# Twelve steps instead of sixteen: two short query tiles of causal attention joined into one step

## The chip, the core and the metric

The kernel runs on one core of a Trainium2 chip. The metric is the device time in microseconds, median of several runs.

## What is computed

The program is two transformer-like layers over 8 batches of 512 tokens of width 128, all in fp32: a recurrent layer with a quantised feed-forward, then an attention with 16 heads and a gated cell. The change lies in the attention of the second layer, whose core is:

```python
nq = _rms(x @ w_cq, g_qnorm)
q = concat(q_nope, rope(q_rope))                       # 16 heads of 96
k1 = concat(ckv @ w_dk_nope, rope(x @ w_krope)/16)     # latent keys
ks, vs = keys and values of the 32 selected tokens
kw, vw = x @ w_wink (rotated), x @ w_winv              # "window" keys
a1 = _attn(q, k1, v1, causal=True)
a2 = _attn(q, ks, vs, causal=False)
a3 = _attn(q, kw, vw, causal=True)
out = (g[:, 0] * a1 + g[:, 1] * a2 + g[:, 2] * a3) @ w_proj
```

A causal softmax over 512 tokens is computed twice per head (a1 and a3), a small one over 32 selected tokens once (a2).

## The kernel before

Heads go in groups of four (HG), so a batch has four groups, and the kernel has 32. The first group runs on its own (FIRST), then a hardware loop of seven turns with four groups each (FULL: groups 1, 2, 3 of a batch and group 0 of the next), then the last three (LAST). Each group has two *rows* (a = 0: a1, a = 1: a3), and each row has 16 *units*: one head h and one query tile t of 128 queries. Tile t sees (t+1) x 128 keys. A row first runs tiles 3 and 2 of its four heads in turn (the tall half), then tiles 1 and 0 (the low half). In row 0, tiles 2, 1 and 0 also compute 32 scores against the selected keys (those of tile 3 ride with tile 0).

Every engine walks through the same numbered steps; step s of PE, DVE and ACT belongs to unit s, with older units at fixed lags, and semaphores join them. What the engines do in step s:

- PE (`attend`, from L1593): the scores of unit s (L1650, L1652) into one of three banks, after the maximum or the exponential of unit s-3; then, at some steps, one set of value matmuls for four heads (`values`, L1612; PV_TALL and PV_LOW say when: four sets for the tall half, two for the low one), or the spreading of the inverted row sums (`spread`, L1623, step SPREAD); then the transposes of unit s-2 (L1672), after its exponential and after the move of unit s-4, whose bank they take; then a *task*, if one is planned.
- DVE (from L1271): a DVE-read task, the masked row maximum of unit s (L1341, which also copies the scores to Pb), the move of unit s-3 out of its bank to PT (L1349, if its tile is moved by DVE), then pieces of the rows (INVERT L1303, NORM L1313, ADD L1322), of the selected softmax (L1282 to L1300), and of the batch.
- ACT (from L875): an ACT-read task, the move of unit s-2 (L886, tile 2 only), the copy of selected scores (L899), the exponential of unit s with its sum (L903), and the move of the spread inverses (L909, step MOVE).

MOVER says who moves which tile: DVE tiles 3, 1 and 0, ACT tile 2. T_LAG is 2, D_LAG is 3.

Tasks share one PSUM bank (7): `group_tasks` (L73) lists at which step of a group which one is filled: nine projections for the next group (x1q, x2q, nq, x1k, x2k, nk3, nk1, vw, vl), the transposed selected probabilities p2T, their product o2, the output projection op of the group before, and for one group in four those of the batch (z4T, gf, gi, gc; cqkv, kr, sel, ks, nqT; vs). A task waits until the one before has been read, and its reader reads it at the start of the next step. POOL rotates queries and keys (`rope`, L633), repeats the inverted row sums (L676), and SP lays the parts of queries and keys with small DMAs (L499). The step numbers of all this were written by hand.

Of the kernel before, what the change touches and what calls it, by code (L numbers as in the profile page):

```python
# [15 lines left out]
P = 128  # L16
B, T = 8, 512
NT = T // P
# [28 lines left out]
HALVES = ((3, 2), (1, 0))  # L47


def units(groups):  # L50

    return [(q, h, a, t) for q in range(groups) for a in range(2) for half in HALVES for h in range(HG) for t in half]

# [19 lines left out]
def group_tasks(q, g, last=False, first=False):  # L73

    steps, proj, extra = {"op": 12, "p2T": 22, "o2": 24}, (0, 2, 4, 7, 8, 13, 15, 17, 19), []
    if g == 0:
        steps, proj = {"op": 11, "p2T": 23, "o2": 25}, (1, 2, 4, 7, 8, 13, 15, 27, 30)
        extra = [] if first else [(17, "z4T"), (20, "gf"), (21, "gi"), (24, "gc")]
    if g == 2 and not last:
        steps, proj = {"op": 11, "p2T": 22, "o2": 24}, (1, 2, 4, 7, 8, 13, 14, 16, 17)  # L80
        extra = [(19, "cqkv"), (23, "kr"), (27, "sel"), (28, "ks"), (30, "nqT")]
    if g == 3 and not last:
        steps, proj = {"op": 11, "p2T": 22, "o2": 24}, (2, 3, 6, 7, 9, 13, 15, 17, 19)
        extra = [(27, "vs")]
# [23 lines left out]
class Turn:  # L108
# [3 lines left out]
    def __init__(self, tasks, i=0):  # L112
# [18 lines left out]
        self.c0 = (NG - 1) * GU if self.first else 0  # L131
# [19 lines left out]
    def col(self, s):  # L151

        q, h, a, t = self.units[s]
        return self.c0 + s - s % RU + (NT - 1 - t) * HG + h
# [10 lines left out]
    def half_free(self, k):  # L165

        r = self.r0 + k // RU
        return r * 2 - 1 if self.units[k][3] >= 2 else r * 2

    def moved(self, k, who):  # L170

        per = sum(MOVER[u[3]] == who for u in units(1))
        if k < 0:
            return self.p0 * per - sum(MOVER[u[3]] == who for u in units(1)[k + 1 + GU:])
        return self.p0 * per + sum(MOVER[u[3]] == who for u in self.units[:k + 1])
# [31 lines left out]
def build(nc, wide_d, mods_d, lat_d, row_d, x_d, out_d):  # L207
    with ExitStack() as ctx:
# [111 lines left out]
        nmax = cv(NG * GU)  # L320
        lsum = cv(NG * GU)
# [147 lines left out]
        def turned(turn, k):  # L469

            _, h, _, t = turn.units[k]
            low, at = int(t < 2), (t % 2 == 0) * P
            return PT[low][:, h, at:].rearrange("p (c x) -> p c x", x=P)[:, 0:2 * t + 1:2]

        def turned_bank(turn, k):
            t = turn.units[k][3]
            return bank[3 + k % 2][:, 0:(t + 1) * P].rearrange("p (c x) -> p c x", x=P)
# [273 lines left out]
        def _(act):  # L751
# [123 lines left out]
            def attend(turn):  # L875
                n_units, u0 = len(turn.units), turn.u0
                p2h = p2.rearrange("p (t j k) -> p j t k", t=NT, j=HG)
                for s in range(turn.n1):
# [4 lines left out]
                    if turn.n0 <= k < n_units and MOVER[turn.units[k][3]] == "act":  # L883
# [3 lines left out]
                    if s < n_units:  # L887
                        q, h, a, t = turn.units[s]
                        n, lo = (t + 1) * P, scores_at(a, t)
                        act.wait_ge(s_max, u0 + (s + 1))  # L890
                        if lo:

                            if turn.g(q) == 1 and s % GU == 1:

                                act.wait_ge(s_c, turn.b + 1)
                            tiles = slice(0, NT, NT - 1) if t == 0 else slice(t, t + 1)
                            m = 2 if t == 0 else 1
                            scores = bank[turn.score_bank(s)][:, 0:m * (KEEP + P)].rearrange("p (m x) -> p m x", m=m)[:, :, 0:KEEP]
                            made = A(p2h[:, h, tiles], scores, ACT.Copy)  # L899
                            if h == HG - 1 and t == 0:  # L900
                                made.then_inc(s_s2, 1)
                        c = turn.col(s)
                        A(Pb[:, s % 4, 0:n], Pb[:, s % 4, 0:n], ACT.Exp, bias=nmax[:, s:s + 1], scale=-1.0,  # L903
                          accum_out=lsum[:, c:c + 1]).then_inc(s_p, 1)
# [5 lines left out]
                    if s < n_units and s % GU == 18:  # L910
                        act.wait_ge(s_s2m, turn.p0 + (s // GU + 1))
                        A(p2, p2, ACT.Exp).then_inc(s_p2, 1)
                    if s < n_units and s % GU == 24 and ("nq", s // GU + 1) in turn.index:
                        selected_keys(turn, s // GU + 1)
# [25 lines left out]
        def _(v):  # L940
# [330 lines left out]
            def attend(turn):  # L1271
# [31 lines left out]
                def row_inverted(r):  # L1303
# [5 lines left out]
                    step(v.reciprocal(inv[:, r % 2], lsum[:, turn.c0 + r * RU:turn.c0 + (r + 1) * RU] if r >= 0 else lsum[:, NG * GU - RU:]))  # L1309
# [19 lines left out]
                for s in range(turn.n1):  # L1329
# [3 lines left out]
                    if s < n_units:  # L1333
                        _, _, a, t = turn.units[s]
                        n, lo = (t + 1) * P, scores_at(a, t)
                        v.wait_ge(s_qk, u0 + (s + 1))
                        if not (turn.first and s < 4):
# [3 lines left out]
                        v.tensor_tensor_reduce(Pb[:, s % 4, 0:n], bank[turn.score_bank(s)][:, lo:lo + n], w("mask", T - n), -1.0, 3e38,  # L1341
                                               ALU.add, ALU.min, nmax[:, s:s + 1]).then_inc(s_max, 1)
                    k = s - D_LAG
                    if turn.n0 <= k < n_units and MOVER[turn.units[k][3]] == "dve":
# [12 lines left out]
                    g = turn.g(q)  # L1357
                    if at == 17:
                        selected_shifted(q)
                    if at == 19:  # L1360
# [418 lines left out]
```

## Time and profile before

| | |
|---|---|
| median of 3 runs | 2321.69 us (2316.57 to 2322.24) |
| profiled execution | 2312.3 us, its span 2310.5 us |
| PE busy | 1911.7 us, 83% |
| DVE busy | 1367.5 us, 59% |
| ACT busy | 1163.8 us, 50% |
| POOL busy | 645.1 us, 28% |
| mean granted TensorE clock | 0.900 |

Busy times overlap between engines. A matmul's end in the trace is modelled, so back-to-back matmuls seem to overlap. "Idle before" is the gap on an engine in front of an instruction, with what ended it.

### The profile page before, as it was taken

What the parts mean: (1) busy time and instruction counts of PE and PEld (TensorE: products, weight loads), DVE (VectorE), ACT (ScalarE), POOL (GpSimd) and SP (SyncE); (2) the same over time, 40 slices, a digit from 0 to 9 for tenths busy, and PEclk for the clock granted to TensorE, in tenths of its full rate; (3) what the DMA queues carried; (4) which work ended last, traced back from release to release, by engine and by line L of the source; (5) the groups of instructions that cost most, each with busy time, mean ns of one, the idle gap of its engine ahead of it and who ended that gap; (6) DMA issues with size and microseconds to landing.
All of it is one profiled execution on the core that took longest, in us unless ns stands there. A gap on an engine that the chain in (4) does not pass through costs nothing.

```text
span 2310.5 us, 40290 instructions
## 1 busy us (share of the span) xinstructions
PE 1911.7 (83%) x10620; PEld 1069.9 (46%) x10620; DVE 1367.5 (59%) x4228; ACT 1163.8 (50%) x3476; POOL 645.1 (28%) x659
## 2 busy tenths in 40 slices
PE   3433357999899998999899989999899899989985
PEld 2221224555445544555455545555455455545542
DVE  5999833656555555555555555555565655565563
ACT  1112213656556565556465655565565556556651
POOL 0323233323323332323232322323232323332200
PEclk7556556999999998989998999899998999899998
DMA  3000002111101110111111111111111111111101
GB/s 137 0 0 0 0 14 53 44 41 36 51 19 40 35 50 23 36 32 40 36 34 36 42 43 33 33 46 42 34 33 45 42 34 33 35 52 31 35 1 37
DMA packets 71349, 81.44 MB, mean 35 GB/s; under 512 B 29521, under 2 KB 37842, under 8 KB 70994
## 3 DMA queue, kind: packets, MB, share of 16 engines
q1 hardware_dynamic: 71122, 78.74, 13.2%
q8 instruction: 102, 1.67, 0.3%
q14 instruction: 125, 1.02, 0.1%
HBM read 7.90 MB, written 2.10 MB: 4 GB/s over the span
## 4 chain that ended last, share of the span: by engine, by line
PE 69%; DVE 17%; issue 8%; ACT 3%; DVEq 1%; POOL 1%; SPq 1%; DMA 0%; ACTq 0%; POOLq 0%
PE bank L1652 21%; PE bank L1672 14%; PE bank L1612 9%; DVE arena L1349 4%; PE bank L1522 4%; PE bank L1523 4%; DVE arena L1341 3%; PE bank L1623 2%; PE bank L1564 2%; PE bank L1545 2%; PE bank L1518 1%; PE bank L1577 1%; PE bank L1560 1%; DVE arena L1106 1%; PE bank L1585 1%
## 5 line engine op out<-in xcount | busy, mean ns | idle before, releaser
L1341 DVE CUSTOM_DVE_ANT_0 arena<-bank,W 128x512 f32<-128x512 f32 (+3 forms) x1024 | 502.0, 490 | 711.4 <-PE bank L1652 573.4
L1652 PE MATMUL bank<-arena 96*128 96x512 f32 (+6 forms) x2048 | 785.6, 466 | 30.8 <-issue 18.3
L903 ACT ACTIVATE arena<-arena 128x512 f32<-128x512 f32 (+3 forms) x1024 | 572.8, 559 | 442.5 <-DVE arena L1341 439.2
L1672 PE MATMUL bank<-W,arena 128*128 128x128 f32 x2560 | 487.1, 288 | 97.1 <-DVE arena L1349 92.0
L1672 PEld LDWEIGHTS bank<-W,arena 128*128 128x128 f32 x2560 | 306.2, 142 | 464.3 <-DVE arena L1349 226.0
L1652 PEld LDWEIGHTS bank<-arena 96*128 96x128 f32 x2048 | 341.1, 199 | 174.6 <-issue 149.7
L1349 DVE COPY arena<-bank 128x512 f32<-128x512 f32 (+2 forms) x768 | 356.2, 464 | 2.0 <-issue 1.5
L685 POOL TENSOR_TENSOR arena<-arena,one 128x512 f32<-128x512 f32 x64 | 66.7, 1042 | 950.6 <-DVE arena L1311 939.7
L1612 PE MATMUL bank<-arena 128*32 128x256 f32 (+1 forms) x3072 | 227.6, 369 | 8.3 <-DVE arena L1349 7.7
L903 ACT ACTIVATION_READ_ACCUMULATOR arena<-arena 128x1 f32 x1024 | 194.8, 190 | 0.0
L886 ACT ACTIVATE arena<-bank 128x384 f32<-128x384 f32 x256 | 125.6, 491 | 116.2 <-PE bank L1672 116.0
L899 ACT ACTIVATE arena<-bank 128x32 f32<-128x32 f32 (+1 forms) x384 | 78.9, 206 | 153.2 <-DVE arena L1341 152.4
L636 POOL TENSOR_TENSOR arena<-arena,W 128x512 f32<-128x512 f32 x64 | 69.8, 1091 | 272.7 <-ACT arena L828 272.7
L1473 PE MATMUL bank<-W,arena 128*128 128x128 f32 x160 | 37.5, 379 | 122.2 <-ACT arena L786 52.7
L1612 PEld LDWEIGHTS bank<-arena 128*32 128x32 f32 x3072 | 61.5, 110 | 166.0 <-issue 128.2
L1522 PE MATMUL bank<-arena,LW 96*128 96x512 f32 x192 | 109.2, 652 | 2.1 <-ACT arena L828 1.4
L1523 PE MATMUL bank<-arena,W 128*128 128x512 f32 x192 | 103.9, 623 | 5.0 <-ACT arena L828 3.6
L645 POOL TENSOR_TENSOR arena<-arena 128x512 f32<-128x512 f32 x64 | 81.4, 1271 | 39.0 <-DMA arena<-arena 31.9
L1473 PEld LDWEIGHTS bank<-W,arena 128*128 128x128 f32 x160 | 26.3, 195 | 135.3 <-ACT arena L786 54.3
L828 ACT ACTIVATE arena<-bank 128x512 f32<-128x512 f32 x128 | 75.6, 590 | 23.5 <-PE bank L1523 8.2
L1341 DVE DVE_READ_ACCUMULATOR2_ANT arena<- 128x1 f32 x1024 | 85.1, 83 | 0.0
L649 POOL TENSOR_TENSOR arena<-arena 128x512 f32<-128x512 f32 x64 | 81.3, 1270 | 5.0
(260 smaller groups left out, 2259.3 us busy)
## 6 DMA issues: line engine op xcount, KB each, us to landing
arena<-arena SPq DMA_DIRECT2D x896, 64.0 KB, 2.0
arena<-arena SPq DMA_DIRECT2D x64, 128.0 KB, 2.4
W<-wide SPq DMA_DIRECT2D x1, 3730.0 KB, 13.3
X<-x SPq DMA_DIRECT2D x8, 256.0 KB, 5.5
out<-arena SPq DMA_DIRECT2D x8, 256.0 KB, 2.2
arena<-arena SPq DMA_DIRECT2D x96, 16.0 KB, 1.9
LW<-lat SPq DMA_DIRECT2D x1, 768.5 KB, 14.3
arena<-mods SPq DMA_DIRECT2D x1, 768.0 KB, 4.5
```

Source lines behind the costliest of these rows:

```text
L645: step(pool.tensor_tensor(stX1, rt[:, 2], rt[:, 3], ALU.subtract))
L649: pool.tensor_tensor(stX2, rt[:, 0], rt[:, 1], ALU.add).then_inc(s_rope, 1)
L886: A(turned(turn, k), turned_bank(turn, k), ACT.Copy).then_inc(s_pa, 1)
L899: made = A(p2h[:, h, tiles], scores, ACT.Copy)
L903: A(Pb[:, s % 4, 0:n], Pb[:, s % 4, 0:n], ACT.Exp, bias=nmax[:, s:s + 1], scale=-1.0, accum_out=lsum[:, c:c + 1]).then_inc(s_p, 1)
L1341: v.tensor_tensor_reduce(Pb[:, s % 4, 0:n], bank[turn.score_bank(s)][:, lo:lo + n], w("mask", T - n), -1.0, 3e38, ALU.add, ALU.min, nmax[: ...
L1349: CP(turned(turn, k), turned_bank(turn, k)).then_inc(s_pd, 1)
L1522: return MM(dst[:], LW[0:QL, col:col + P], latT[0:QL], start=True, stop=True)
L1523: return MM(dst[:], w("wink", col, P), hTc, start=True, stop=True)
L1612: last = MM(bank[5][rows, low * 2 * P:low * 2 * P + n], V[a][turn.g(q) % 2][:, c, rows], PT[low][:, h, c * 2 * P:c * 2 * P + n], start=(c ...
L1652: MM(bank[turn.score_bank(s)][:, 0:lo + n], query(t), Kb[a][0:QD, g % 2, h, skip:skip + lo + n], start=True, stop=True).then_inc(s_qk, 1)
L1672: last = pe.transpose(bank[3 + k % 2][:, c * P:(c + 1) * P], Pb[:, k % 4, c * P:(c + 1) * P], ident)
```

## The change

Tiles 1 and 0 of a head become one unit: their scores lie side by side in one bank (`laid`), two maxima and two exponentials follow each other in its step, its three transposed blocks are put in an order that lets one copy of 384 elements move them, and tile 2 is now moved by DVE as well, so that ACT moves none. A row has 12 steps and a group 24. The lag of the DVE move is two steps instead of three. The steps of value matmuls, row pieces and all tasks are numbered anew.

```diff
-HALVES = ((3, 2), (1, 0))
+STEPS = ((3,), (2,)), ((1, 0),)
...
+def laid(a, tiles):
+
+    at, out = 0, []
+    for t in reversed(tiles):
+        lo = scores_at(a, t)
+        out.append((t, (t + 1) * P, lo, at))
+        at += lo + (t + 1) * P + (lo if t == 0 else 0)
+    return out[::-1]
...
-T_LAG, D_LAG = 2, 3
-PV_TALL, PV_LOW = 11, 19
-INVERT, SPREAD, MOVE, NORM, ADD = 16, 19, 21, 23, 24
-MOVER = {3: "dve", 2: "act", 1: "dve", 0: "dve"}
+T_LAG, D_LAG = 2, 2
+PV_TALL, PV_LOW = 10, 14
+INVERT, SPREAD, MOVE, NORM, ADD = 12, 14, 15, 16, 17
+MOVER = {3: "dve", 2: "dve", 1: "dve"}
...
-    steps, proj, extra = {"op": 12, "p2T": 22, "o2": 24}, (0, 2, 4, 7, 8, 13, 15, 17, 19), []
+    steps, proj, extra = {"op": 8, "p2T": 18, "o2": 20}, (0, 2, 4, 6, 7, 9, 11, 13, 15), []
     if g == 0:
-        steps, proj = {"op": 11, "p2T": 23, "o2": 25}, (1, 2, 4, 7, 8, 13, 15, 27, 30)
-        extra = [] if first else [(17, "z4T"), (20, "gf"), (21, "gi"), (24, "gc")]
+        steps, proj = {"op": 7, "p2T": 18, "o2": 20}, (0, 1, 3, 5, 6, 9, 10, 21, 22)
+        extra = [] if first else [(12, "z4T"), (14, "gf"), (15, "gi"), (19, "gc")]
     if g == 2 and not last:
-        steps, proj = {"op": 11, "p2T": 22, "o2": 24}, (1, 2, 4, 7, 8, 13, 14, 16, 17)
-        extra = [(19, "cqkv"), (23, "kr"), (27, "sel"), (28, "ks"), (30, "nqT")]
+        proj = (0, 1, 3, 5, 6, 9, 10, 11, 12)
+        extra = [(15, "cqkv"), (17, "kr"), (19, "sel"), (21, "ks"), (22, "nqT")]
...
         def turned(turn, k):
 
-            _, h, _, t = turn.units[k]
-            low, at = int(t < 2), (t % 2 == 0) * P
-            return PT[low][:, h, at:].rearrange("p (c x) -> p c x", x=P)[:, 0:2 * t + 1:2]
+            _, h, _, tiles = turn.units[k]
+            if tiles[0] == 1:
+                return PT[1][:, h]
...
# ACT, step s
+                        for t, n, lo, at in laid(a, tiles):
+                            c = turn.col(s, t)
+                            here = Pb[:, s % 4, at_p:at_p + n]
+                            done = A(here, here, ACT.Exp, bias=nmax[:, c:c + 1], scale=-1.0, accum_out=lsum[:, c:c + 1])
+                            at_p += n
+                        done.then_inc(s_p, 1)
...
# PE, step s
+                        for t, n, lo, at in laid(a, tiles):
+                            skip = 0 if lo or a else KEEP
+                            last = MM(B_[:, at:at + lo + n], query(t), Kb[a][0:QD, g % 2, h, skip:skip + lo + n],
+                                      start=True, stop=True)
...
-                        for c in range(t + 1):
-                            last = pe.transpose(bank[3 + k % 2][:, c * P:(c + 1) * P], Pb[:, k % 4, c * P:(c + 1) * P], ident)
+                        order = (0, 2, 1) if tiles[0] == 1 else range(tiles[0] + 1)
+                        for n, c in enumerate(order):
+                            last = pe.transpose(bank[3 + k % 2][:, n * P:(n + 1) * P], Pb[:, k % 4, c * P:(c + 1) * P], ident)
```

On DVE the selected softmax moves from steps 17, 19, 20, 21 to 13, 15, 16, 17; for the batch, the tokens from 20 to 23 to 13 to 16, the picks (L1220) from 24 to 17, norm_latents from 28 to 20, the statistics from 13 to 9, normed_out (L1252) from 16 to 11, the cell from 26 to 29 to 21 to 23.

## Rows read from the trace of the kernel before

**Rows 1.** The row maxima by their line: count, shortest/median/longest ns, first and last start.

```profile
L1341 DVE CUSTOM_DVE_ANT_0 arena<-bank,W x1024: 282/485/693, 379.8 to 2255.5; 128x512 f32<-128x512 f32 x86, 128x256 f32<-128x256 f32 x85
```

**Rows 2.** Four groups of a turn: us; busy PE, PEld, DVE, ACT, POOL; clock.

```profile
1143.70:1199.10 55.40, 51.65 (x302) 28.29 (x302) 31.21 (x103) 32.53 (x98) 15.65 (x14) 0.96 0.14 34
1199.10:1265.60 66.50, 61.78 (x349) 36.96 (x348) 36.98 (x120) 36.40 (x119) 21.91 (x20) 0.90 0.12 30
1265.60:1319.70 54.10, 50.52 (x311) 27.69 (x309) 31.48 (x103) 33.46 (x102) 15.64 (x14) 1.00 0.20 47
1319.70:1384.50 64.80, 57.52 (x316) 31.42 (x316) 36.72 (x123) 34.91 (x102) 18.36 (x20) 0.94 0.14 38
```

**Rows 3.** The chain of waits in the third group (1265.6 to 1319.7), shares by line.

```profile
by line: PE bank L1652 26.1%; PE bank L1672 20.1%; PE bank L1612 11.2%; issue 7.5%; DVE arena L1349 6.4%; PE bank L1523 4.8%; PE bank L1522 4.8%; DVE arena L1341 4.3%; PE bank L1623 2.2%; PE bank L1564 2.0%; PE bank L1518 1.9%; PE bank L156
```

**Rows 4.** Waits of one turn (1143.7 to 1384.5): us in total, times, longest.

```profile
PE bank L1672 <- DVE arena L1349: 11.2, 23, 2.3
...
PE bank L1652 <- issue: 3.0, 1, 3.0
```

**Rows 5.** Timeline of PE in the third group: start, us, instructions, idle before.

```profile
1302.17 0.81 PE L1652 MATMUL bank<-arena 96*128 96x384 f32 x2
1302.82 0.49 PE L1672 MATMUL bank<-W,arena 128*128 128x128 f32 x3
1303.15 1.02 PE L1652 MATMUL bank<-arena 96*128 96x512 f32 x2
...
1311.52 0.44 PE L1672 MATMUL bank<-W,arena 128*128 128x128 f32 x2 [1.11 <-DVE arena L1349]
...
1312.11 0.64 PE L1612 MATMUL bank<-arena 128*32 128x256 f32 x8
1312.68 0.33 PE L1672 MATMUL bank<-W,arena 128*128 128x128 f32 x1
```

**Rows 6.** Groups of instructions by shape, third group: busy us, mean ns, idle before.

```profile
L1672 PE MATMUL bank<-W,arena 128*128 128x128 f32 x81 | 15.3, 285 | 2.9 <-DVE arena L1349 2.8
...
L1341 DVE CUSTOM_DVE_ANT_0 arena<-bank,W 128x512 f32<-128x512 f32 x9 | 6.2, 690 | 7.5 <-PE bank L1652 4.5 <-PE bank L1672 2.9
L903 ACT ACTIVATION_READ_ACCUMULATOR arena<-arena 128x1 f32 x32 | 6.1, 189 | 0.0
...
L1349 DVE COPY arena<-bank 128x512 f32<-128x512 f32 x8 | 5.5, 686 | 0.0
...
L903 ACT ACTIVATE arena<-arena 128x256 f32<-128x256 f32 x8 | 4.0, 504 | 2.3 <-DVE arena L1341 2.2
L886 ACT ACTIVATE arena<-bank 128x384 f32<-128x384 f32 x8 | 3.9, 490 | 3.3 <-PE bank L1672 3.3
...
L1341 DVE CUSTOM_DVE_ANT_0 arena<-bank,W 128x256 f32<-128x256 f32 x8 | 3.4, 422 | 3.7 <-PE bank L1652 3.7
L1349 DVE COPY arena<-bank 128x256 f32<-128x256 f32 x8 | 3.4, 420 | 0.0
...
L903 ACT ACTIVATE arena<-arena 128x128 f32<-128x128 f32 x8 | 3.2, 397 | 1.3 <-DVE arena L1341 1.3
...
L1341 DVE CUSTOM_DVE_ANT_0 arena<-bank,W 128x128 f32<-128x128 f32 x8 | 2.3, 292 | 3.7 <-PE bank L1652 2.8 <-PE bank L1672 0.9
L1349 DVE COPY arena<-bank 128x128 f32<-128x128 f32 x8 | 2.3, 286 | 0.1
```

**Rows 7.** Timeline of POOL in the first group: the two rotations.

```profile
1150.68 1.09 POOL L636 TENSOR_TENSOR arena<-arena,W 128x512 f32<-128x512 f32 x1 [4.57 <-ACT arena L828]
...
1156.46 1.28 POOL L649 TENSOR_TENSOR arena<-arena 128x512 f32<-128x512 f32 x1
...
1164.93 1.27 POOL L645 TENSOR_TENSOR arena<-arena 128x512 f32<-128x512 f32 x1 [0.48 <-DMA arena<-arena]
```

**Rows 8.** Timeline: the picks of the second group, z4T of the fourth.

```profile
1244.18 2.42 DVE L1220 TENSOR_SCALAR arena<-W,rankT 128x32 f32<-128x32 f32 x4
...
1351.33 0.63 PE L1473 MATMUL bank<-W,arena 128*128 128x128 f32 x4 [2.15 <-DVE arena L1252]
```

More of the change, by code:

```diff
@@ L469, in turned @@
         def turned(turn, k):
[L471 to L473 removed]
+            _, h, _, tiles = turn.units[k]
+            if tiles[0] == 1:
+                return PT[1][:, h]
+            return PT[0][:, h, (tiles[0] == 2) * P:].rearrange("p (c x) -> p c x", x=P)[:, 0:2 * tiles[0] + 1:2]
         def turned_bank(turn, k):
[L476 to L477 removed]
+            tiles = turn.units[k][3]
+            blocks = bank[3 + k % 2][:, 0:sum(t + 1 for t in tiles) * P]
+            return blocks if tiles[0] == 1 else blocks.rearrange("p (c x) -> p c x", x=P)
         block = ctx.enter_context(nc.Block())
@@ L882, in attend @@
                     k = s - T_LAG
-                    if turn.n0 <= k < n_units and MOVER[turn.units[k][3]] == "act":
+                    if turn.n0 <= k < n_units and MOVER[turn.units[k][3][0]] == "act":
                         act.wait_ge(s_pT, u0 + (k + 1))
@@ L1333, in attend @@
                     if s < n_units:
-                        _, _, a, t = turn.units[s]
-                        n, lo = (t + 1) * P, scores_at(a, t)
+                        _, _, a, tiles = turn.units[s]
                         v.wait_ge(s_qk, u0 + (s + 1))
@@ L1340, in attend @@
                         v.sem_inc(s_seen, 1)
-                        v.tensor_tensor_reduce(Pb[:, s % 4, 0:n], bank[turn.score_bank(s)][:, lo:lo + n], w("mask", T - n), -1.0, 3e38,
-                                               ALU.add, ALU.min, nmax[:, s:s + 1]).then_inc(s_max, 1)
+                        at_p = 0
+                        for t, n, lo, at in laid(a, tiles):
+                            c = turn.col(s, t)
+                            last = v.tensor_tensor_reduce(Pb[:, s % 4, at_p:at_p + n],
+                                                          bank[turn.score_bank(s)][:, at + lo:at + lo + n],
+                                                          w("mask", T - n), -1.0, 3e38, ALU.add, ALU.min, nmax[:, c:c + 1])
+                            at_p += n
+                        last.then_inc(s_max, 1)
                     k = s - D_LAG
-                    if turn.n0 <= k < n_units and MOVER[turn.units[k][3]] == "dve":
+                    if turn.n0 <= k < n_units and MOVER[turn.units[k][3][0]] == "dve":
                         v.wait_ge(s_pT, u0 + (k + 1))
@@ L1627, in attend @@
                     if s < n_units:
-                        q, h, a, t = turn.units[s]
-                        g, n = turn.g(q), (t + 1) * P
+                        q, h, a, tiles = turn.units[s]
+                        g = turn.g(q)
                         if s % GU == 0:
```

118 lines of the change are left out of this document (59 added, 59 removed).

## The prediction

> **What bounds the kernel now.** I read the page first: PE is busy 83% of the span, DVE 59%, ACT 50%. That makes TensorE the suspect, but a busy PE is a modelled figure, so I asked where the row maxima of the attention run. They run from 379.8 to 2255.5 us, 1024 of them [rows 1]: 1876 of the 2310.5 us are the stage the change touches. I then cut one turn of the batch loop at the first row maximum of each group of heads [rows 2]. The four groups last 55.4, 66.5, 54.1 and 64.8 us, sum 240.8. The second also prepares the next batch's selected tokens and latents, the fourth runs the layer norm and the cell; the first and third are plain. The third is the cleanest: granted clock 1.00 throughout, PE 50.5 of 54.1 us, DVE only 31.5, ACT 33.5.
>
> So is the plain group bound by matmuls? Its chain of waits says: mostly. Lines of PE carry it, but DVE L1349 (moving a turned block) has 6.4%, DVE L1341 (the row maximum) 4.3% and "issue" 7.5% [rows 3]. Together that is 18.2% of 54.1, or 9.8 us in which the path leaves PE. The waits of the whole turn show the shape: the transposes of L1672 wait for the move of L1349, 23 times and 11.2 us, the longest 2.3 [rows 4]. The timeline shows one of them: 1.11 us of idle PE in front of two transposes, ended by L1349 [rows 5].
>
> Why do they wait? Transposed blocks go to two banks in turn, so the transposes of unit k need the move of k-2. PE issues the transposes of k in step k+2; VectorE moves k-2 in step k+1, behind the maximum of k+1. PE thus has one score matmul between the maximum's input and its own need, VectorE a maximum and a move: 0.69 + 0.69 us for a 512-wide tile [rows 6]. Any odd piece on VectorE goes straight to PE.
>
> **The change, part by part.**
>
> Steps. A row of attention (4 heads, 4 query tiles) goes from 16 steps to 12, a group from 32 to 24. Score columns, transposes, value matmuls and their weights stay the same in number and size, so PE's own work stays. Within a joined step two maxima and two exponentials follow each other; their number stays too. What goes is 8 rounds of waits per group.
>
> Moves. Per head and row VectorE had 512, 256 and 128 elements: 0.686 + 0.420 + 0.286 = 1.39 us, ScalarE 384 in 0.490 [rows 6]. Now VectorE moves 512, 384 and 384. No DVE copy of 384 stands in the trace. The three sizes lie on a line of 0.153 us plus 1.04 ns an element, which gives 0.55; the bounds are the 256 and the 512 copy, 0.42 and 0.69. The new sum is 0.686 + 2 x 0.55 = 1.79, +0.40, and with eight head-rows +3.2 us of VectorE per group (1.1 to 5.4 by the bounds). VectorE goes from 31.5 to 34.7 us in a plain group, ScalarE (eight moves less) from 33.5 to 29.5. Neither is full.
> The Trainium skill (VectorE: DVE Perf Modes, its section on the TRN2 errata) prices a VectorE pass out of PSUM at 120 cycles plus one per element at 0.96 GHz. An estimate from it is 0.525 us for 384, which would lower VectorE's load by 16 x 0.03 = 0.4 us per group against my line; no row here has the size.
>
> The lag. The move of k-2 now runs in step k, a step earlier, and PE needs it in step k+2: a whole step lies between. The transposes' waits for L1349 should go. In the plain group, idle PE in front of L1672 is 2.9 us [rows 6]. But a modelled matmul end lies later than the next one could start: scores began at 1302.17 and are drawn 0.81 long, yet the transposes behind them began at 1302.82 [rows 5], so each wait hides 0.16 us more. With some nine waits, those of values and p2T among them (some 0.5 us, an estimate from the 1.11 of a long one), that is 2.9 + 0.5 + 9 x 0.16 = 4.8 us. Shorter waits hide wholly in that tail; the chain's 9.8 us is the bound for all, and I take 1.6 us of the remaining 5.0. Gone: 6.4 us a group, bounds 2.9 and 9.8.
>
> What is late next. I laid the 24 steps of a plain group end to end, in the order of the code's waits. PE's prices come from start to start in the timeline [rows 5]: 384 columns of scores 0.65 us, so 1.69 ns a column, 0.86 for tile 3 or a projection, 0.70 or 0.65 for tile 2; three transposes 0.33, so 0.11 each; values of 256 columns 0.57. A joined unit has 480 or 384 columns, 0.81 or 0.65; its short matmuls need as many weight loads as long ones, so I take 0.95 and 0.75.
> - Steps 16 to 18. VectorE has a maximum and a move in each (1.38, 1.12, 1.38 us), in 16 also the row's normalisation and a small reciprocal, in 17 the scaling of the selected probabilities; a pass over 512 is 0.69 by the nearest rows, the small one I take at 0.3 [rows 6]. With step 16's scores issued at 0, the scaling ends near 5.5; p2T, which needs it, stands in step 18, where PE arrives at 4.0. Wait about 1.6 us.
> - Steps 21 and 22. The tall values of the second row now begin the step after their last move. In 21 VectorE first adds o2 (0.69), then takes a joined maximum (0.42 + 0.29) and the move (0.55); PE, with no task in 21, arrives about 1.2 us early. The first row has nk3 in step 9 as cover and waits for nothing.
> - Step 7. x2k follows x1k directly. ScalarE reads x1k only when POOL has finished the rotation of q, 7.1 us from its first operation to the end of its last [rows 7], and that starts no earlier than now: about 0.6 us. Low values in step 2: 0.1.
> Together 3.5 us; with sequencer gaps on VectorE, which I did not lay, 4.1. Bounds: zero, if PE's own seams cover them, and 8 us.
> Joined steps lengthen the way from scores to probabilities: 0.42 + 0.29 on VectorE, then 0.50 + 0.19 + 0.40 + 0.19 on ScalarE [rows 6], some 3.9 us with the selected scores and the handovers. Two steps of PE, with the third's scores in front, give 4.1 us at the barest place (steps 20 to 22). It just holds.
> POOL, SP and DMA: the second rotation still waits for the laid parts of the first (its store at 1164.93, 7.2 us after the first ended at 1157.74 [rows 7]) and ends near 27 us, before the repeat of the row sums (28) and the spread (30). The lays end near 39 us of a group of 52. No wait.
>
> Odd groups. In the second, the four picks of 2.42 us [rows 8] move from step 24 to 17, beside the scaling; cqkv, kr, p2T, sel, o2, ks and nqT share one bank in eight steps. Their readers sit in ScalarE's and VectorE's order, and VectorE still waits in line for ks. In the fourth, z4T still waits for normed_out (2.15 us now [rows 8]) and VectorE reaches it some 0.8 us before POOL's deviation is there. The loop's turn costs PE 3.0 us [rows 4] as before. The new waits on banks at a loop's start ask for one unit more than they must; the units asked for are long done. I take 2 us gained in each, as the same transposes' waits go.
>
> The sum: plain group 6.4 - 4.1 = 2.3 us, odd group 2.0 to 2.3; over 32 groups 32 x 2.3 = 74 us. The profiled execution took 2312.3 us (span 2310.5) and the median of the runs is 2321.7, 9 us more. A difference carries over: span near 2237, and 2321.7 - 74 = **2248 us**.
>
> **The rivals.**
> *The new waits are covered.* Everything named under "late next" was laid without PE's small seams; if PE is 0.15 us later per step, p2T and the values find their inputs. Then 4.5 to 5 us a group stay: 32 x 4.6 = 147, **2175 us**. For it: VectorE and ScalarE both stay under 70%. There is also clock to win: the second group ran at a mean grant of 0.90, the first and fourth at 0.96 and 0.94 [rows 2], the lower of 1.2 and 2.4 GHz in the thin stretches. Against it: DVE work is now in fewer, fuller steps.
> *Slower: VectorE in series with PE.* VectorE takes the maximum of s, then sits in the move of s-2 until PE has issued that unit's transposes in the same step, and only then can take the maximum of s+1; move and values also tie PE to it in 22, 23 and 14. In steps 12 to 23 VectorE has about 20 us of work where PE has 21. If a handover costs 0.25 us on each of two instructions more in these twelve steps, that is 3 us a group over my 4.1, and with the packed bank 7 of the odd groups the account turns: it decides once the new waits pass 6.4 us. At 7.0 us: +0.6 x 32 = 19, **2341 us**.
> The Trainium skill (Perfetto Trace Analysis, the section on optimizing Scalar/DVE operations) speaks for this one: it says that grouping helps where the engine is saturated, but that where unsaturated engines cause bubbles on another, breaking instructions up may let work finish sooner. The trace agrees with its premise (DVE 58% busy in a plain group); the change goes the other way, and by the rule the latency would be worth more than the rounds saved.
> *Nothing moves:* the stall leaves L1349 and comes back at p2T and the values in full, **2322 us**.
>
> **How the numbers follow.** My sum, 2215 to 2285: 0.54. Covered waits, 2160 to 2215: 0.22. No change: 0.08. Slower: 0.16. Times under 2175 and over 2330 take some 0.18 of it, so the range is 2175 to 2330. A measurement tells 0.3% (7 us) from no change. Faster 0.77, same 0.07, slower 0.16.
>
> **What would show it.** In the new trace, transposes waiting for the move should be nearly gone, with waits in front of p2T's transposes and of the second row's first values in their place; a plain group near 51.8 us; DVE copies of 384 near 0.55 us; DVE near 35 us a group; no copy by ScalarE from the transposed banks. I am wrong if plain groups stay at 54 or more with VectorE waiting for transposes (series), or if ScalarE's exponentials, not the maximum or the move, end PE's waits (the latency of joined steps). The odd groups are the weakest part: I laid them by likeness only.

## The result, and the profile after

The changed kernel takes 2165.0 us (median of four runs, 2152.5 to 2174.9) against 2322.0 for the kernel before: a ratio of 0.933, 95% interval 0.928 to 0.938. The forecast was 2248, with a range from 2175 to 2330. The sign was right; the gain, 157 us, is twice the 74 forecast. The profiled spans differ by 147 us (2310.5 and 2163.4).

The first part of the page, then the row maxima by line (to set beside [rows 1]):

```profile
span 2163.4 us, 38682 instructions
PE 1812.5 (84%) x10620; PEld 1073.2 (50%) x10620; DVE 1465.2 (68%) x4228; ACT 1029.9 (48%) x3220; POOL 654.4 (30%) x659
...
L1364 DVE CUSTOM_DVE_ANT_0 arena<-bank,W x1024: 284/460/695, 380.1 to 2106.8; 128x512 f32<-128x512 f32 x86, 128x256 f32<-128x256 f32 x85
```

The attention stage (first to last start of a row maximum) went from 1875.8 to 1726.7 us, 149 less, so all of the gain lies there. One turn cut at the first row maximum of each group, with the columns of [rows 2] (us; busy PE, PEld, DVE, ACT, POOL; clock; DMA share; GB/s):

```profile
1087.45:1138.70 51.25, 47.88 (x297) 28.06 (x296) 35.36 (x102) 28.20 (x90) 15.97 (x14) 0.97 0.15 38
1138.70:1198.00 59.30, 57.12 (x356) 35.56 (x348) 38.31 (x119) 32.35 (x111) 21.92 (x20) 0.94 0.14 34
1198.00:1249.50 51.50, 47.90 (x316) 28.51 (x308) 35.40 (x102) 29.39 (x94) 15.99 (x14) 1.00 0.21 49
1249.50:1308.90 59.40, 54.46 (x327) 31.47 (x320) 39.47 (x123) 30.89 (x94) 18.82 (x20) 1.00 0.15 42
```

Here is the surprise. The third group, the plain one on which the prediction was built, went from 54.1 to 51.5: the forecast was 51.8. The second lost 7.2 us and the fourth 5.4, where "2 us gained in each" was forecast. The waits of PE in the third group (total us, times, longest) are the three that the prediction named, and none for the move in front of a transpose, where [rows 4] had 23 in a turn:

```profile
PE bank L1549 <- ACT arena L844: 1.5, 1, 1.5
PE bank L1595 <- DVE arena L1320: 1.3, 1, 1.3
PE bank L1638 <- DVE arena L1375: 0.7, 1, 0.7
```

VectorE's shapes in the same group show the new copy of 384 at 555 ns:

```profile
L1375 DVE COPY arena<-bank 128x384 f32<-128x384 f32 x16 | 8.9, 555 | 2.0 <-PE bank L1702 1.8
...
L1375 DVE COPY arena<-bank 128x512 f32<-128x512 f32 x8 | 5.5, 687 | 1.6 <-PE bank L1702 1.6
```

The picks and the pieces of normed_out over the whole run, before (L1220, L1252) and after (L1241, L1273); mean ns is the second number behind the bar:

```profile
L1220 DVE TENSOR_SCALAR arena<-W,rankT 128x32 f32<-128x32 f32 x32 | 17.6, 615 | 0.0
L1252 DVE TENSOR_SCALAR arena<-X,small 128x128 f32 x28 | 14.4, 575 | 0.0
```

```profile
L1273 DVE TENSOR_SCALAR arena<-X,small 128x128 f32 x28 | 7.7, 340 | 0.0
...
L1241 DVE TENSOR_SCALAR arena<-W,rankT 128x32 f32<-128x32 f32 x32 | 5.4, 233 | 0.0
```

The same instructions on the same shapes take 0.38 and 0.59 of their former time, though nothing was done to them but to move them. The clock changed as well: 0.90 became 0.94 in the second group, 0.94 became 1.00 in the fourth. A mean of 0.90 over a group says that TensorE ran a fifth of it at 1.2 instead of 2.4 GHz; such time is called half clock below.

The theory that I took from this: three causes add up. The lag removes a wait in every group; picks and normed_out no longer meet GpSimd (POOL); and the clock, which fell behind those stalls, holds. Rivals: the joined steps themselves pay more than I laid, or the bunches of small instructions were the trouble, not where they stood.

### The profile page after: what moved, and what is told of

Its sections match the earlier page's. It is cut to its first block, busy times and chain, and to the rows that moved or that the text cites. A ratio compares the mean times of both kernels' runs of the same rounds, so it can differ in the third digit from the quotient of the medians.

```text
span 2163.4 us, 38682 instructions
## 1 busy us (share of the span) xinstructions
PE 1812.5 (84%) x10620; PEld 1073.2 (50%) x10620; DVE 1465.2 (68%) x4228; ACT 1029.9 (48%) x3220; POOL 654.4 (30%) x659
## 4 chain that ended last, share of the span: by engine, by line
PE 64%; DVE 14%; issue 13%; POOL 4%; ACT 3%; SPq 1%; DMA 0%; DVEq 0%; POOLq 0%; ACTq 0%
PE bank L1675 21%; PE bank L1702 11%; PE bank L1638 8%; PE bank L1548 3%; PE bank L1549 3%; DVE arena L1364 2%; PE bank L1649 2%; PE bank L1590 1%; PE bank L1586 1%; PE bank L1544 1%; PE bank L1603 1%; DVE arena L1127 1%; DVE arena L1375 1%; PE bank L1611 1%; PE bank L1612 1%
## 5 line engine op out<-in xcount | busy, mean ns | idle before, releaser
L1364 DVE CUSTOM_DVE_ANT_0 arena<-bank,W 128x512 f32<-128x512 f32 (+3 forms) x1024 | 480.2, 487 | 437.9 <-PE bank L1675 297.5
L1675 PE MATMUL bank<-arena 96*128 96x512 f32 (+6 forms) x2048 | 718.9, 453 | 24.2 <-issue 14.7
L1375 DVE COPY arena<-bank 128x384 f32<-128x384 f32 (+1 forms) x768 | 460.1, 599 | 90.2 <-PE bank L1702 83.0
L1675 PEld LDWEIGHTS bank<-arena 96*128 96x128 f32 x2048 | 353.0, 193 | 200.9 <-issue 172.5
L1702 PE MATMUL bank<-W,arena 128*128 128x128 f32 x2560 | 428.3, 281 | 0.7 <-ACT arena L923 0.6
L1702 PEld LDWEIGHTS bank<-W,arena 128*128 128x128 f32 x2560 | 300.3, 143 | 220.3 <-issue 187.3
L1638 PE MATMUL bank<-arena 128*32 128x256 f32 (+1 forms) x3072 | 220.8, 360 | 13.2 <-DVE arena L1375 10.4
L917 ACT ACTIVATE arena<-bank 128x32 f32<-128x32 f32 (+1 forms) x384 | 65.1, 204 | 200.6 <-DVE arena L1364 199.7
L1638 PEld LDWEIGHTS bank<-arena 128*32 128x32 f32 x3072 | 60.9, 108 | 196.7 <-issue 154.9
L1499 PE MATMUL bank<-W,arena 128*128 128x128 f32 x160 | 36.4, 369 | 107.4 <-ACT arena L802 52.8
L661 POOL TENSOR_TENSOR arena<-arena 128x512 f32<-128x512 f32 x64 | 81.6, 1274 | 48.0 <-DMA arena<-arena 42.8
L665 POOL TENSOR_TENSOR arena<-arena 128x512 f32<-128x512 f32 x64 | 85.9, 1342 | 5.0
L1499 PEld LDWEIGHTS bank<-W,arena 128*128 128x128 f32 x160 | 24.9, 187 | 120.1 <-ACT arena L802 54.4
L601 POOL TENSOR_TENSOR small<-small,epsc 128x4 f32<-128x4 f32 x24 | 4.9, 203 | 219.0 <-DVE small L977 219.0
```

The source lines that it names most:

```text
L661: step(pool.tensor_tensor(stX1, rt[:, 2], rt[:, 3], ALU.subtract))
L665: pool.tensor_tensor(stX2, rt[:, 0], rt[:, 1], ALU.add).then_inc(s_rope, 1)
L1364: last = v.tensor_tensor_reduce(Pb[:, s % 4, at_p:at_p + n], bank[turn.score_bank(s)][:, at + lo:at + lo + n], w("mask", T - n), -1.0, 3e3 ...
L1375: CP(turned(turn, k), turned_bank(turn, k)).then_inc(s_pd, 1)
L1638: last = MM(bank[5][rows, low * 2 * P:low * 2 * P + n], V[a][turn.g(q) % 2][:, c, rows], PT[low][:, h, c * 2 * P:c * 2 * P + n], start=(c ...
L1675: last = MM(B_[:, at:at + lo + n], query(t), Kb[a][0:QD, g % 2, h, skip:skip + lo + n], start=True, stop=True)
```

## The experiments

All ratios are to the kernel before, run on the same chip, with 95% intervals. This table has the mean length of the four groups of a turn over the seven turns of the loop, from the starts of the row maxima in the one trace of each kernel:

| kernel | us | ratio | 1st | 2nd | 3rd | 4th |
|---|---|---|---|---|---|---|
| before | 2322.0 | 1 | 55.0 | 65.9 | 54.1 | 64.1 |
| before, lag 2 | 2181.8 | 0.939 (0.933 to 0.944) | 48.8 | 60.8 | 48.7 | 64.4 |
| before, lag 2, tile 2 by DVE | 2215.8 | 0.954 (0.951 to 0.958) | 49.3 | 63.1 | 49.8 | 64.8 |
| before, lag 2, z4T later | 2172.1 | 0.933 (0.927 to 0.938) | 49.1 | 63.9 | 48.6 | 60.5 |
| before, picks one a step | 2280.4 | 0.981 (0.979 to 0.983) | 55.0 | 61.4 | 54.1 | 64.6 |
| before, both out of POOL's way | 2261.5 | 0.974 (0.969 to 0.979) | 55.2 | 60.9 | 54.1 | 61.7 |
| before, normed_out alone | 2302.0 | 0.992 (0.989 to 0.994) | 54.9 | 67.8 | 54.1 | 61.2 |
| before, picks in another form | 2283.4 | 0.986 (0.983 to 0.989) | 55.0 | 60.1 | 54.1 | 65.0 |
| before, lag 2 and both moves | 2137.1 | 0.925 (0.918 to 0.932) | 49.0 | 58.9 | 48.7 | 59.6 |
| after | 2165.0 | 0.933 (0.928 to 0.938) | 50.7 | 58.0 | 51.8 | 59.4 |
| after, picks at 18 | 2164.5 | 0.933 (0.929 to 0.937) | 50.9 | 57.8 | 51.8 | 59.4 |
| after, tile 2 by ACT | 2129.1 | 0.917 (0.914 to 0.920) | 49.5 | 57.9 | 49.6 | 58.1 |
| after, three tasks moved | 2149.4 | 0.925 (0.923 to 0.928) | 50.3 | 58.4 | 50.1 | 59.2 |
| both of these | 2126.0 | 0.915 (0.914 to 0.917) | 49.3 | 57.7 | 49.2 | 58.2 |
| after, tile 2 by ACT, tasks anew | 2107.4 | 0.909 (0.907 to 0.911) | 48.7 | 56.8 | 48.7 | 58.3 |

### The parts of the change one by one

The kernel before with the shorter lag and nothing else:

```diff
-T_LAG, D_LAG = 2, 3
+T_LAG, D_LAG = 2, 2
```

> The kernel before with one change: VectorE moves a turned block two steps back instead of three. If the lag is the main part of the gain (theory lag), the transposes' waits for the move (11.2 us a turn of the loop before) fall under 2 us, plain groups go from 54.1 to about 51 us, and the time to 2200 to 2240 us. If the joined steps are the main part (theory join), the short steps of tiles 1 and 0 leave VectorE waiting for the transposes of the same step, plain groups stay above 53 us, and the time above 2280 us.

Measured: 2181.8 us, 140 of the 157. The third group falls by 5.4 us, the measured size of what the prediction called gone (6.4). The fourth gains nothing (64.1 to 64.4).

The same with tile 2 moved by VectorE:

```diff
-MOVER = {3: "dve", 2: "act", 1: "dve", 0: "dve"}
+MOVER = {3: "dve", 2: "dve", 1: "dve", 0: "dve"}
```

> The kernel before with the lag of two steps and with tile 2 moved by VectorE too; the steps are not joined and the tasks stay. If moving the copy to VectorE helps because ScalarE's exponentials no longer stand behind it, this is 10 to 30 us faster than the lag alone. If VectorE's extra 3 to 4 us a group cost what they free, it is within 7 us of the lag alone or slower. What is left to 2165 us is then the joined steps and the new task steps: theory join expects over 80 us left, theory lag under 50.

Measured: 2215.8, 34 us worse. The reverse edit on the changed kernel (`MOVER = {3: "dve", 2: "act", 1: "dve"}`):

> The changed kernel with tile 2 moved by ScalarE as before. If the move to VectorE was a gain, this is 10 to 30 us slower; if VectorE is what PE waits for in the groups (p2T 1.42 us, values 0.83 us a group), taking eight copies of 0.6 us off it makes this 10 to 40 us faster.

Measured: 2129.1, 36 us better. So this part of the change is a loss of 34 to 36 us in either kernel, and the prediction had it at nothing. With it on VectorE, value matmuls wait for the moves: in the unjoined kernel a wait comes up (in the whole run) that its ACT twin does not have among its longest.

```profile
PE bank L1612 <- DVE arena L1349: 25.6, 23, 1.7
```

The changed kernel with the old lag (D_LAG 3):

> The changed kernel with the move three steps back again. Theory lag: most of the gain goes, 2165 to 2240 us or more, waits of the transposes for the move come back (over 10 us a turn) and the half-clock stretches with them. Theory join: longer steps give VectorE time for either lag, under 2190 us.

Measured: ratio 1.052 (1.045 to 1.059), slower than the kernel before; the ratio is that of two runs at 2430.0 and 2454.1 us, two more took 2476.9 and 2481.6, and the trace is of one of these. The move comes a step late for the values, all over the run:

```profile
PE bank L1638 <- DVE arena L1375: 197.5, 123, 2.3
```

So the joined kernel pays only with the shorter lag. By subtraction the rest, joined steps with their newly laid tasks, brings 52 us: 2181.8 to 2129.1 with tile 2 on ScalarE, 2215.8 to 2165.0 on VectorE. The table says where: 2.9 and 6.3 us in the second and fourth group, nothing in the plain ones (0.7 and 0.9 worse).

### Is it the joining, or where the picks and normed_out stand?

First the two places one by one. The picks of the kernel before spread over steps 23 to 26:

> The kernel before with one thing changed: the four picks of the second group, 2.42 us in step 24, go one each to steps 23 to 26. Theory picks: the wait of 2.42 us in that group and the half-clock stretch of 13 to 17 us that begins 2 us later both come from this bunch; the group goes from 65.9 to about 60 us and the time falls by 35 to 50 us. Rival: the bunch is worth its own wait only, about 1.5 us a turn, 10 us in all, and the stretch of half clock stays because the small matmuls of sel and ks make it.

Measured: 2280.4, 43 less than its neighbour on the same chip (2323.9); the picks take 302 ns on average, and the second group 61.4 us. Then z4T a step later, on top of lag 2:

> The kernel before with the lag of two steps, and the task z4T of the fourth group one step later (18 instead of 17). Lag alone left the fourth group at 64.4 us while the changed kernel has 59.4; theory z4T says that the wait for normed_out (2.98 us) and the half-clock stretch behind it are that difference: the wait falls under 1 us, the group to about 61 us, the time by 15 to 30 us against the lag alone. Rival: the difference lies in the end of the loop's turn (4.1 us) and in the cell, and this kernel is within 7 us of the lag alone.

Measured: 2172.1. The 10 us under lag 2 alone are not clear of the spread (the intervals 0.927 to 0.938 and 0.933 to 0.944 overlap). In the traces the fourth group gains 3.9 us and the second loses 3.1: less waiting in one place, and more half clock in another (5.9 us a second group became 13.2). Neither run says why the picks were slow. The timeline of the kernel before does, beside [rows 8]:

```profile
1244.39 1.12 POOL L654 TENSOR_TENSOR arena<-arena,W 64x512 f32<-64x512 f32 x1 [4.79 <-ACT arena L823]
...
1245.47 1.08 POOL L655 TENSOR_TENSOR arena<-arena,W 64x512 f32<-64x512 f32 x1
```

The bunch started at 1244.18. The four picks (shortest, median, longest ns):

```profile
L1220 DVE TENSOR_SCALAR arena<-W,rankT x4: 234/656/1130, 1244.2 to 1245.5; 128x32 f32<-128x32 f32 x4
```

Two took 0.23 us, and each of the last two took as long as one GpSimd instruction. That asks for a test by place: the bunch kept together, but at a step where GpSimd is through, and normed_out likewise.

```diff
-                    if g == 2 and at == 24:
+                    if g == 2 and at == 26:
...
-                        if at == 16:
+                        if at == 15:
```

> The kernel before, with two things moved in its odd steps and nothing else: the bunch of four picks stands at step 26 instead of 24, and normed_out at step 15 instead of 16, where GpSimd has no tensor_tensor in hand at the same time. Theory (a pick or a z4 piece of VectorE is held up while GpSimd works, because the two share a way to SBUF): the bunch of picks costs 4 x 0.233 = 0.93 us instead of 2.42, the z4 pieces 340 ns instead of 575, the wait for z4T falls from 2.4 us to near nothing, the half clock behind both places shrinks, the second group takes about 60 us instead of 65.9 and the fourth about 61.5 instead of 64.1: 50 to 70 us off, 2255 to 2275. Rival (the bunch itself, or the small matmuls around it, costs the time): the pieces keep 575 ns and the picks 500 to 600, and the time stays within 15 us of 2322. If b_pick (the picks one a step, 2280) had its gain from spreading alone, this one lies above it by 20 us or more.

Measured: 2261.5 us, 57 less than its neighbour on the same chip (2318.4), and a bunch of 0.67 us. The picks, then normed_out and z4T:

```profile
1229.44 1.26 POOL L659 TENSOR_TENSOR arena<-arena 64x512 f32<-64x512 f32 x1 [0.17 <-POOL arena L655]
1230.53 0.67 DVE L1220 TENSOR_SCALAR arena<-W,rankT 128x32 f32<-128x32 f32 x4
...
1322.19 1.10 DVE L1252 TENSOR_SCALAR arena<-X,small 128x128 f32 x4
...
1325.01 0.63 PE L1473 MATMUL bank<-W,arena 128*128 128x128 f32 x4
```

The POOL row is nearly over when the picks begin, and z4T no longer waits. The time, the groups (60.9 and 61.7) and the pieces (340 ns) came as the theory had them; the bunch is shorter than its 0.93 us, because picks of 235 ns start 0.15 us apart. Place, not bunching, made them slow. normed_out alone (step 15):

> The kernel before with normed_out one step earlier (15 instead of 16) and nothing else. Theory (its pieces are held up while GpSimd works): 340 instead of 575 ns a piece, the wait for z4T in the fourth group of a turn goes from 2.4 us to 1 or less, that group takes 61.5 us instead of 64.1, and the second group stays at 65.9: 10 to 25 us off, 2295 to 2310. Rival (all of the gain of the two moves together came from the picks): within 7 us of 2320.

Measured: 2302.0, ratio 0.992 (0.989 to 0.994). So about 19 of the 57 us belong to it, and by subtraction the rest to the picks; as above, part of what the fourth group gains (2.9) goes over to the second (1.9 lost).

Then the form. Each pick of the kernel before as a tensor_tensor, at its old step:

```diff
-return TS(onehot[:, j], w("iota"), rankT[:, j, ds(b, 1)], None, ALU.is_equal)
+return TT(onehot[:, j], w("iota"), rankT[:, j, ds(b, 1)].to_broadcast([P, KEEP]), ALU.is_equal)
```

> The kernel before with the picks at their old step, but each a tensor_tensor (row of numbers against the rank, broadcast) instead of a tensor_scalar; same place, same result. It tells what of VectorE is held up while GpSimd works. If it is only the form with one tensor operand and both ends in SBUF (tensor_scalar): 220 to 300 ns a pick, the second group at 61 us, and 2275 to 2290 us in all. If any instruction of VectorE on SBUF is held up: 450 to 650 ns a pick and the time within 10 us of 2320.

Measured: 2283.4, which is what "tensor_scalar alone is held up" gave. But the trace does not say so:

```profile
L1220 DVE TENSOR_TENSOR arena<-W,rankT x4: 185/187/1083, 1235.3 to 1235.6; 128x32 f32<-128x32 f32 x4
```

The fourth pick is held up as before, 1083 ns against GpSimd's 1.13 us. The form is only shorter (0.19 us instead of 0.23), so three were through before GpSimd began, and one such wait is met instead of two. The time agreed with a theory whose mechanism is wrong; without that row I would have carried it off. The Trainium skill (SBUF — State Buffer, section "Who interferes with whom") says that VectorE and GpSimd share a pair of ports, that whichever starts first holds it for its whole instruction while the other fully blocks, and that this goes for tensor_scalar in a two-port mode and for tensor_tensor with both inputs in SBUF against GpSimd's reads. The rows above agree on both: 1130 and 1083 ns, where a GpSimd instruction took 1.08 to 1.13 us. Which port it is, no run here shows. And not every GpSimd instruction holds VectorE up. In the changed kernel with tile 2 on ScalarE all 28 picks of the loop begin while GpSimd has a power over 128x8 elements in hand (L682, drawn 1.66 us long), in its last 0.57 us, and they take 233 ns on average:

```profile
1162.13 1.66 POOL L682 TENSOR_TENSOR small<-small,cst 128x8 f32<-128x8 f32 x1
...
1163.22 0.67 DVE L1241 TENSOR_SCALAR arena<-W,rankT 128x32 f32<-128x32 f32 x4
```

So the rule of the Trainium skill, that the other fully blocks, does not show in these rows. Either the power was through with SBUF by then, or its drawn end is too late; no run tells which.

The half clock is the other half of it. These two second groups are both of the kernel before with lag 2:

```profile
475.70:534.00 58.30, 54.71 (x350) 33.24 (x349) 37.22 (x119) 35.86 (x119) 21.91 (x20) 1.00 0.14 33
697.43:761.56 64.13, 60.74 (x349) 37.77 (x349) 37.43 (x120) 36.10 (x119) 21.91 (x20) 0.89 0.13 31
```

The code is the same, and one ran (1 - 0.89) x 64.13 x 2 = 14 us at 1.2 GHz. That costs 5.8 us, 0.41 us for each us at the lower level. The kernel before gives nearly the same: its second groups took 60.9 us at a clock of 1.00 and 68.0 at 0.875. The pick experiment shows that a small stall can start it: in the second group of b_pick_tt (the picks as tensor_tensor) the bunch is 1.0 us shorter, and the group is

```profile
1190.13:1250.12 59.99, 55.69 (x349) 32.53 (x349) 35.91 (x119) 36.35 (x119) 21.92 (x20) 1.00 0.13 33
```

against 66.50 at 0.90 in [rows 2]. By 0.41, the 13 us of half clock there are 5.5 of the 6.5 us. Over the seven turns, six second groups had half clock in the kernel before (12.2 us each on average), and one in b_pick_tt (0.5).

### What joining brings by itself

Lag 2 and both moves in the unjoined kernel:

> The kernel before with D_LAG 2 and the same two moves (picks at step 26, normed_out at step 15). Theory: groups of 48.8, 58.3, 48.7 and 60.5 us, where D_LAG 2 alone had 48.8, 60.8, 48.7 and 64.4: 2115 to 2135. It says what the joined steps bring by themselves: the joined kernel with tile 2 moved by ScalarE takes 2129. If joining pays beside the better order of tasks, this one stays at 2150 or above; if the gain of the joined steps was only that their picks and z4 pieces stand elsewhere, it comes down to 2130 or below.

Measured: 2137.1, 7 us above the line I had drawn. So of the 52 us, the medians give about 45 to where the picks and normed_out stand, and 8 are left to the joined steps with their renumbered tasks (2137.1 to 2129.1). The four runs of this kernel lie 30 us apart (2131.4 to 2161.3); by the ratios, which compare with the kernel before on the same chip, it is 31 and 18 us. The first of the two is clear of noise (0.933 to 0.944 against 0.918 to 0.932); in the second the intervals overlap (0.918 to 0.932, 0.914 to 0.920): no difference is shown. The reverse test, the picks of the changed kernel at step 18, beside GpSimd:

> The kernel after with its four picks one step later, at step 18, where GpSimd works on the shared key. Theory (held up by GpSimd): the picks take 500 to 600 ns each instead of 233, a wait of 1 to 1.5 us comes up in the steps behind them, and in some of the second groups half clock with it: 10 to 50 us more, 2175 to 2215. Rival (place does not matter, the picks were slow in the kernel before for their bunching among small matmuls): 233 ns as before and within 7 us of 2165.

Measured: 2164.5, no change. The hold is there:

```profile
1183.60 1.08 POOL L670 TENSOR_TENSOR arena<-arena,W 64x512 f32<-64x512 f32 x1 [1.06 <-ACT arena L839]
1184.16 1.91 DVE L1241 TENSOR_SCALAR arena<-W,rankT 128x32 f32<-128x32 f32 x4
...
1186.21 1.05 PE L1568 MATMUL bank<-arena 128*128 128x32 f32 x8 [1.00 <-DVE arena L1241]
```

The bunch takes 1.91 us again, and sel waits 1.0 us for it. Yet the second groups last 57.8 us on average against 58.0. This one, at a clock of 1.00, took 56.6, and the changed kernel's second groups at 1.00 took 56.2: the hold by itself costs 0.4 us. Four of seven second groups had half clock in the changed kernel (59.3 us each), three of seven here. My expectation of 10 to 50 us was wrong: held-up picks cost much only where the clock falls behind them. What makes it fall here, or not, is open. It also means that the 45 us hold for the unjoined kernel alone: in the joined one the place of the picks is worth nothing that can be measured, and normed_out was not put back.

Last, the waits that the joined kernel made for itself. In the groups 1 and 3, p2T at 19, o2 at 21, x2k at 8 and op at 7, in the changed kernel and then with tile 2 on ScalarE:

> The changed kernel with task steps of the two plain groups of a turn altered: p2T 18 to 19, o2 20 to 21, x2k 7 to 8, op 8 to 7. If the new waits at p2T (1.42 us) and x2k (1.61 us) are what the prediction took them for, they mostly go: plain groups from 51.4 to about 48.7 us, the time by 16 x 2.7 = 43 us to about 2120. If VectorE paces the plain groups, the waits only move to the values or the transposes and the time stays within 10 us.

> The changed kernel with tile 2 moved by ScalarE and the same task steps altered. The waits at p2T and x2k are 0.96 and 1.17 us there: if they go, plain groups fall from 49.6 to about 47.7 us and the time by 25 to 35 us from 2129 to about 2100. If they only move, within 7 us of 2129.

Measured: 2149.4 and 2126.0. The first gains 16 us, the second 3, inside the noise: with ScalarE moving tile 2, VectorE reaches p2T's input in time anyway. The wait for x2k only went on to the task behind it, op (22.6 us in the first of the two runs, 15.9 in the second):

```profile
PE bank L1606 <- ACT arena L847: 22.6, 15, 1.5
```

So op went in front of x1k, and the odd groups were laid anew too:

> The kernel after with tile 2 moved by ScalarE and tasks laid anew: in the plain groups, op at step 6, x1k 7, x2k 8, p2T 19, o2 21, and in the odd ones p2T 19, o2 21, vw 20, vl 22 and gc 18. Theory (what the joined step left are waits for x2k, p2T and the values, each for a result that VectorE gets to late): the waits for x2k 1.6 and p2T 1.4 us go, a plain group takes 48.3 us instead of 51.8 (of which 2.3 are tile 2), the odd ones about 57: 2090 to 2110. Rival (the waits only move to the next task, as op did when x2k was laid later): within 7 us of 2126.

Measured: 2099.1; it is left out of the table, because it computes something else. In this order gc writes its result over the selected probabilities before p2T has read them, so part of the selected attention is computed from other values; the instructions are the same. With p2T and gc in their old order:

> As the last version (tile 2 moved by ScalarE, tasks laid anew), but in the groups with the output tasks p2T stays at step 18 and gc at 19, since gc's result goes where p2T still reads its input; o2 21, vw 20 and vl 22 as there. Theory (the waits for x2k, p2T and the values were the joined step's own): the plain groups take 48.5 us and the odd ones 56.6 and 57.3, 2095 to 2105 us, 25 us below the version with only three tasks moved (2126). Rival (the waits only move on): within 7 us of 2126.

Measured: 2107.4, ratio 0.909 (0.907 to 0.911), the best kernel of the study, 58 us under the changed one; this was 2 us above what I expected. Its turn:

```profile
1065.09:1114.01 48.92, 48.40 (x300) 28.79 (x300) 30.96 (x94) 31.10 (x98) 16.08 (x14) 0.98 0.16 39
1114.01:1170.12 56.11, 54.01 (x356) 33.49 (x348) 34.56 (x112) 35.37 (x119) 21.90 (x20) 1.00 0.14 35
1170.12:1218.87 48.75, 48.13 (x316) 28.53 (x308) 31.21 (x94) 32.15 (x102) 16.09 (x14) 1.00 0.22 53
1218.87:1277.60 58.73, 54.82 (x324) 31.15 (x316) 35.59 (x115) 33.86 (x102) 18.78 (x20) 0.98 0.16 42
```

It is 30 us under the best unjoined kernel, but that one's tasks were not laid anew, so how much of the 30 is joining stays open. The plain groups are equal (48.7 us).

## Why the prediction was right and wrong

The whole gain, from the medians: lag -140, picks and normed_out in other places about -45, joined steps about -8 (not told from nothing), tile 2 to VectorE +36. Sum -157, as measured. By the ratios the four are -143, -31, -18 and +36. These are the steps of one path, in this order; in another order the two in the middle could share otherwise. By group, as differences of the table's rows (us):

| step | 1st | 2nd | 3rd | 4th |
|---|---|---|---|---|
| lag 2 | -6.2 | -5.1 | -5.4 | +0.3 |
| picks and normed_out moved | +0.2 | -1.9 | 0.0 | -4.8 |
| steps joined, tasks renumbered | +0.5 | -1.0 | +0.9 | -1.5 |
| tile 2 to VectorE | +1.2 | +0.1 | +2.2 | +1.3 |
| sum | -4.3 | -7.9 | -2.3 | -4.7 |

- *The plain group* was right as a result: 51.8 forecast, 51.8 on average. Gone was 5.4 instead of 6.4. The three waits were forecast at 1.6, 1.2 and 0.6, and measured 1.3 (p2T), 0.7 (values) and 1.5 (x2k): 3.5 in sum, both times. x2k was undersized by 0.9, the values and p2T oversized by 0.5 and 0.3.
- *The odd groups*, "I take 2 us gained in each ... by likeness only", are the step that failed. They gained 7.9 and 4.7 on average. Over the 2.3 us a group of the sum that is 5.6 and 2.4 more, in seven turns 56 of the 75 us by which the stage's gain of 149 exceeds 74. Two things were wrong in the term. First, it took over the plain group's loss of 4.1 us to new waits beside the gain of the lag. In the second group the lag brought 5.1 us, and joining and tile 2 together took nothing of it back (-1.0 and +0.1). Second, I moved the bunch of picks at 2.42 us and normed_out at its price in the old place, as if these were their own. They cost 0.67 and 1.10 by themselves. In the fourth group this is all of the gain: the lag alone brought nothing there, since PE only waited longer for normed_out (24.7 us in the run instead of 20.0), and the two moves brought 4.8. Both rows were on the table; what I did not ask was why a 128x32 pass takes 0.6 us when a 128x128 copy takes 0.29 [rows 6].
- *The clock* was named only inside a rival ("there is also clock to win"), without a price. Half clock fell from 12.2 to 3.9 us in the mean second group and from 6.4 to 0.8 in the fourth: at 0.41, an estimate of 3.4 and 2.3 us of what these gained.
- *The first groups* gained 4.3, and 2.3 was forecast. With lag 2 alone they gained 6.2, and joining and tile 2 took 1.7 back, not 4.1. Half clock fell there by only 0.7 us; why less was late than in the third group I did not pursue.
- *Tile 2* was costed at +3.2 us of VectorE and "neither is full". The load was right (555 ns a copy against 0.55 forecast, 35.4 us a group against 35), the conclusion wrong: it cost 0.4 to 2.3 us in a group of the unjoined kernel, and 0.1 to 2.2 in the joined one, where p2T waits 31.5 us in the run instead of 19.9. An engine that is 69% busy over a group is still full in the steps where the values wait for it. That the lag itself is worth more hid this error. The estimate of 0.525 us for this copy, worked out from the figures of the Trainium skill (VectorE: DVE Perf Modes, the section on the TRN2 errata), lies 5% below the 0.555 measured.
- *The rivals.* "Covered waits" gave 2175 and came nearest, but its mechanism did not occur: the waits were there in full. That 2165 lies in its band (2160 to 2215) is luck. "VectorE in series" is half true, since a part of it sits in the 35 us of tile 2, but it did not decide. The old lag with joined steps, at 1.052, is the slower case in the flesh: the values then wait for the move.
- *The range* ended at 2175 because it was made of plain-group terms times 32. A part "laid by likeness" should have had bounds of its own: its whole stall (2.42 + 2.15 us and the half clock of [rows 2]) on the one side, nothing on the other.

## What to carry to other kernels

Before an instruction's price is carried to a new place, compare it with others of its kind and size: if it is two or three times dearer, read the timeline of the other engines over it, because the price may belong to the place. Where a stage has stretches of half clock, price a removed stall together with the clock behind it, and ask of each group of the loop on its own; a likeness to the cleanest group holds only for groups as clean. And undo the parts of a compound change one by one, even if it wins: here the largest part was one digit, and another part lost 35 us.

## What the runs showed of the hardware

- A VectorE tensor_scalar or tensor_tensor on SBUF that begins while one of GpSimd's tensor_tensors over 512 elements (or a 128x128 one) is under way can be stretched to about that instruction's length: 0.23 to 1.13 us for a 128x32 tensor_scalar, 0.19 to 1.08 for a tensor_tensor of the same size, 0.34 to 1.06 for a 128x128 piece of normed_out. Copies out of PSUM beside GpSimd kept their 0.69 and 0.55 us, and picks beside the power over 128x8 their 0.23.
- The changed kernel made a hold of its own: the row's addition, an SBUF tensor_tensor of 512, took 687 ns on average before and 1022 after. In the third group it ran beside the rotation, whose last instruction took 1.60 us instead of 1.28: first VectorE loses, then GpSimd's next instruction. With tile 2 on ScalarE the addition took 763 ns on average and the rotation's last instruction 1.27 (an earlier one of it 1.54 instead of 1.09 in the one row read), so this may be part of the 36 us there; in the unjoined kernel tile 2 cost 34 us with the addition at 681 ns. No run changed this alone.

```profile
1209.94 1.10 POOL L663 TENSOR_TENSOR arena<-arena,W 128x512 f32<-128x512 f32 x1
1210.10 1.49 DVE L1347 TENSOR_TENSOR arena<-arena 128x512 f32<-128x512 f32 x1
1211.11 1.60 POOL L665 TENSOR_TENSOR arena<-arena 128x512 f32<-128x512 f32 x1
```

- A stall of some 1 us can bring 13 us at 1.2 GHz behind it, and each of these cost 0.41 us; but it need not, as the picks at step 18 and one second group of the kernel before (clock 1.00) show. And a removed stall in one group can come with more half clock in another (normed_out alone: 4th group -2.9 us, 2nd +1.9, with half clock up from 12.2 to 16.6 us).
